# The experts' down products with the weights stationary and the output transposed and turned back

## Chip, cores and metric

The kernel runs on one core of one Trainium2 chip. The metric is device time in microseconds (us) of one execution; a kernel's time is the median of its runs. TensorE is called PE, VectorE DVE, ScalarE ACT, GpSimd POOL and SyncE SP.

## The reference, cut to what matters

The whole network is a graph convolution, a mixture of experts, an attention over edges and a second small mixture, on 10,000 tokens of 512 numbers. The change touches the first mixture only. There each of 32 experts takes the 312 tokens (k) that rank highest for it, and four experts share one up matrix:

```python
k = min(int(bs * C_CAP) // E, bs)                      # 10000 // 32 = 312
G_ek, idx_ek = jax.lax.top_k(Sm.T, k)
tokens = xf[idx_ek]
up = jnp.einsum('gjkh,ghf->gjkf', tok_g, W_up) + b_up[:, None, None, :]
act = jax.nn.silu(up).reshape(E, k, D_FF)              # D_FF = 1365
Eout = jnp.einsum('ekf,efh->ekh', act, W_down) + b_down[:, None, :]
weighted = G_ek[..., None] * Eout
y = jnp.zeros((bs, H), dtype=x.dtype).at[idx_ek.reshape(-1)].add(weighted.reshape(-1, H))
```

## The kernel before

`experts` works through the experts one after another. The 312 tokens of an expert are held as three parts (Q = 3) of 104 (S), the 512 features as four chunks (C = 4) of 128, and the 1365 hidden features as eleven tiles (M = 11), ten of 128 and one of 85. Every product is made of three matmuls, since each operand is split into a high and a low part.

The engines run their own loops and meet by semaphores. `tiles` gives each engine a list of stages with a lag; eight experts at the start and some at the end are written out, and twenty in the middle run in a hardware loop of four experts to a pass, five passes.

For an expert e the work on each engine is:

- PE: `up(e)`: for each hidden tile m, 12 matmuls with `up_hi` or `up_lo` stationary and 312 tokens moving, into one of U = 3 buffers of `psU`. Then `down(e)`: for each m, 9 matmuls with 104 tokens of `hid_hi` or `hid_lo` stationary and 512 features of `dn_hi` or `dn_lo` moving, into `psO`, which holds the three parts. Down is cut into B = 4 batches of hidden tiles (3, 3, 3, 2); behind each of the first three comes one `turn` of the next expert, which transposes 104 gathered tokens into `psT`, a tile of two buffers.
- ACT: `raise_parts(e+1)` makes `x_hi` and `dn_hi` for the next expert during `down(e)`; the `dn_hi` of a batch waits for this expert's down products of that batch, the last one for the end of down. Then `activate(e+1)`: two SiLU activations per hidden tile, one to `hid_hi`, one to `hid`.
- DVE: `lower_parts(e+1)` makes `x_lo` and `dn_lo` behind ACT; then `locate(e+2)`, eight small instructions in a chain that find the token numbers of a later expert; then `weigh(e)`, which reads `psO`, adds the bias `bdn` (the expert's row copied to all partitions) and multiplies by the gate; then `split(e+1)`, eleven subtractions that make `hid_lo`.
- POOL issues the gathers of tokens and the scatter of `y`; SP issues the loads of weights, and of `bdn`, one per expert.

The order on DVE is set by the list of stages alone, `[(0, stage), (2, prepare), (2, lower_parts), (1, locate), (3, weigh), (2, split)]`, and is strict. ACT waits before tile m for `hid_low` of tile m - 4, as `hid` has four buffers. PE waits before up tile m for the activations of tile m - U.

Of the kernel before, what the change touches and what calls it, by code (L numbers as in the profile page):

```python
# [10 lines left out]
ALU = mybir.AluOpType  # L11
# [1171 lines left out]
def experts(nc, g, K, tile_of, rest, row, W_up, b_up, W_down, b_down):  # L1183
# [14 lines left out]
    width = [min(P, F - m * P) for m in range(M)]  # L1198
    U = 3
    L = 2 * Q + 2  # L1200
# [8 lines left out]
    with Phase(nc, "experts") as ph:  # L1209
# [8 lines left out]
        bup = ph.sb("bup", [P, X // GR, M])  # L1218
        bdn = ph.sb("bdn", [P, 2, D])
        y = ph.sb("y", [P, 2, Q, D])  # L1220
# [12 lines left out]
        psU = ph.ps("psU", [P, U, 512])  # L1233
        psO = ph.ps("psO", [P, Q, 512])
        gm, gx, scattered = ph.sems("gm", 2), ph.sems("gx", 2), ph.sems("scattered", 2)
        up_loaded, dn_loaded, bias_loaded, biases = ph.sems("up_loaded", C), ph.sems("dn_loaded", 2), \
            ph.sems("bias_loaded", 2), ph.sem("biases")
        staged, located, turned, x_high, x_low, up_high, up_low, dn_high, dn_low, upped, activated = (
# [5 lines left out]
        @block.sync  # L1244
        def _(sp):
            for m in range(M):
                sp.dma_start(bup[0:width[m], :, m:m + 1],
                             b_up[:, m * P:m * P + width[m]].rearrange("g (p o) -> p g o", o=1),
                             allow_slow_non_contiguous=True).then_inc(biases, 16)
            up_rows = W_up.rearrange("g h f -> (g h) f")  # L1250
            down_rows = W_down.rearrange("e f h -> (e f) h")

            def load(e, j):
                if j == 0:
                    for c in range(C):
                        if not isinstance(e, int) or e >= GR:
                            sp.wait_ge(up_low, (e - GR) * (C // GR) + c + 1)
                            sp.sem_inc(waited, 1)
                        sp.dma_start(up_raw[:, c, :], up_rows[bass.ds(e * (D // GR) + c * P, P), :])\
                            .then_inc(up_loaded[c], 16)  # L1260
                for k in range(B):
                    if not isinstance(e, int) or e * B + k >= 2:
                        sp.wait_ge(dn_low, e * B + k - 1)
                        sp.sem_inc(waited, 1)
                    whole = [m for m in batch[k] if m < FULL]
                    sp.dma_start(dn_raw[:, k % 2, 0:len(whole), :],
                                 down_rows[bass.ds(e * F + whole[0] * P, len(whole) * P), :]
                                 .rearrange("(m p) h -> p m h", p=P)).then_inc(dn_loaded[k % 2], 16)
                    if batch[k][-1] == M - 1:
                        sp.dma_start(dn_raw[0:width[-1], k % 2, len(whole), :],  # L1270
                                     down_rows[bass.ds(e * F + FULL * P, F - FULL * P), :]).then_inc(dn_loaded[k % 2], 16)
                at_least(sp, out_step, e, 2, 2 * Q)
                sp.sem_inc(waited, 1)
                sp.dma_start(bdn[:, j % 2, :], b_down[bass.ds(e, 1), :].rearrange("o h -> (o h)").partition_broadcast(P))\
                    .then_inc(bias_loaded[j % 2], 16)
            tiles(sp, X, [(0, load)], R)

        @block.gpsimd
        def _(pool):
# [20 lines left out]
            def scatter(e, j):  # L1300


                at_least(pool, out_step, e, 0, 2 * Q)
                pair_landed(pool, scattered, e, j, Q, 1)
# [9 lines left out]
        def _(pe):  # L1314
            def turn(e, j, q):

                if q == 0:
                    pair_landed(pe, gx, e, j, Q)
                if not isinstance(e, int) or e * Q + q >= 2:
                    pe.wait_ge(x_low, e * Q + q - 1)  # L1320
                for c in range(C):
                    mm = pe.transpose(psT[:, (j * Q + q) % 2, c * S:(c + 1) * S],
                                      xg[0:S, j % 2, q, c * P:(c + 1) * P], g.ident[0:S, 0:S])
                mm.then_inc(turned, 1)

            def up(e, j):
# [4 lines left out]
                for m in range(M):  # L1331
# [3 lines left out]
                    for c in range(C):  # L1335
                        pe.matmul(acc, up_hi[:, c, cols], x_hi[:, c, :], start=(c == 0), stop=False)  # L1336
                        pe.matmul(acc, up_hi[:, c, cols], x_lo[:, c, :], start=False, stop=False)  # L1337
                        mm = pe.matmul(acc, up_lo[:, c, cols], x_hi[:, c, :], start=False, stop=(c == C - 1))  # L1338
                    mm.then_inc(upped, 1)

            def down(e, j):
                at_least(pe, out_step, e, 1, 2 * Q)
                for k in range(B):
                    pe.wait_ge(dn_low, e * B + k + 1)
                    for m in batch[k]:
                        pe.wait_ge(hid_low, e * M + m + 1)
                        w = width[m]
                        for q in range(Q):
                            s = slice(q * S, (q + 1) * S)
                            pe.matmul(psO[0:S, q, :], hid_hi[0:w, m, s], dn_hi[0:w, m, :], start=(m == 0), stop=False)  # L1350
                            pe.matmul(psO[0:S, q, :], hid_hi[0:w, m, s], dn_lo[0:w, m, :], start=False, stop=False)  # L1351
                            mm = pe.matmul(psO[0:S, q, :], hid_lo[0:w, m, s], dn_hi[0:w, m, :],  # L1352
                                           start=False, stop=(m == M - 1))
                        mm.then_inc(downed, 1)
                    if k < Q and not (isinstance(e, int) and e == X - 1):
                        turn(e + 1, (j + 1) % R, k)
            for q in range(Q):
                turn(0, 0, q)
            tiles(pe, X, [(1, up), (1, down)], R)

        @block.scalar
        def _(act):
# [10 lines left out]
            def raise_parts(e, j):  # L1373


                for k in range(B):
# [5 lines left out]
                    if not isinstance(e, int) or e >= 1:  # L1382
                        act.wait_ge(downed, (e - 1) * M + batch[k][-1] + 1)
                    act.copy(dn_hi[:, batch[k][0]:batch[k][-1] + 1, :], dn_raw[:, k % 2, 0:len(batch[k]), :])\  # L1384
                        .then_inc(dn_high, 1)

            def activate(e, j):

                for m in range(M):
# [4 lines left out]
                    if not isinstance(e, int) or e >= 1:  # L1394
# [4 lines left out]
                                   bias=bup[0:width[m], bass.ds(e // GR, 1), m]).then_inc(activated, 1)  # L1399
            tiles(act, X, [(0, prepare), (0, raise_parts), (0, activate)], R)  # L1400

        @block.vector
        def _(v):
            chain = Chain(v, located, L)
            outs = Chain(v, out_step, 2 * Q)

# [12 lines left out]
            def locate(e, j):  # L1419
                chain.at(e)  # L1420
                pair_landed(v, gm, e, j, Q)
                pair_landed(v, scattered, e, j, Q, 4)
                at_least(v, out_step, e, R, 2 * Q)
                for q in range(Q):
# [8 lines left out]
                chain.end()  # L1433

            def weigh(e, j):
                k = j % 2
                outs.at(e)
                pair_landed(v, bias_loaded, e, j, 1)
                pair_landed(v, scattered, e, j, Q, 2)
                at_least(v, downed, e, 0, M)  # L1440
                for q in range(Q):
                    outs(v.tensor_tensor(y[0:S, k, q, :], psO[0:S, q, :], bdn[0:S, k, :], ALU.add))
                    outs(v.tensor_scalar(y[0:S, k, q, :], y[0:S, k, q, :], gate[0:S, j, q:q + 1], None, ALU.mult))  # L1443
                outs.end()
# [14 lines left out]
            def split(e, j):  # L1459

                for m in range(M):
# [754 lines left out]
```

## Time and profile before

| | us |
|---|---|
| median of 3 runs | 4214.27 (4212.77 to 4214.78) |
| the profiled execution | 4210.74 |
| its span, first to last instruction | 4209.0 |
| PE busy | 3413.8 (81%) |
| DVE busy | 2659.6 (63%) |
| POOL busy | 1414.7 (34%) |
| ACT busy | 1239.1 (29%) |
| mean granted clock of PE | 0.89 |

The profile's page gives busy times by engine, the span in 40 slices of equal length, and groups of instructions by line. The trace behind it gives the start and duration of each instruction, what ended the idle time ahead of it, and sums over any stretch. A granted clock of 1.00 is PE's upper level, 2.4 GHz, and 0.50 its lower, 1.2 GHz; a value between is a mean over a stretch that has both. Durations of matmuls are modelled and overlap; the distance of their starts tells what one costs in a stream. `experts` is the stretch from about 1690 to 3110 us.

### The profile page before, as it was taken

Reading aid. Unit: us, or ns where it says so; the run is one execution under the profiler, and the core shown is the slowest. Engines: PE = TensorE matmul, PEld = TensorE weight load, DVE = VectorE, ACT = ScalarE, POOL = GpSimd, SP = SyncE. Lnnn points to the kernel's source line nnn. Section 1 sums busy time; section 2 is a strip of 40 time slices with the busy share of each in tenths; the row PEclk is TensorE's granted clock in tenths of the full one; section 3 lists DMA queues with packets and bytes.
Section 4 is the critical chain, followed back from the end, with each engine's and each line's share of the span. In section 5 each row is a group of like instructions: output and inputs, shape, how many; then the busy total and the mean of one; then the engine's idle time right before and its main releaser. Section 6 shows DMA issues by size and latency. Waiting matters only on the chain. (4 is left out here: it accounts for less than half of the span.)

```text
span 4209.0 us, 60863 instructions
## 1 busy us (share of the span) xinstructions
PE 3413.8 (81%) x16811; PEld 2667.0 (63%) x16812; DVE 2659.6 (63%) x6025; ACT 1239.1 (29%) x2287; POOL 1414.7 (34%) x1753
## 2 busy tenths in 40 slices
PE   4876377888877410899999999999949996688999
PEld 3610255666677410788888888888838884575766
DVE  7765797894367677454544545445428887776776
ACT  0122144452211100443443434344311111113443
POOL 0176387783255201132222222223113330006552
PEclk9999699999955555899999999999979998798999
DMA  1043222333399401454544534445322210126664
GB/s 51 0 126 80 63 93 83 110 97 120 118 310 310 150 0 36 131 143 102 144 124 113 134 102 137 128 107 142 95 71 60 58 55 17 74 94 147 160 156 107
DMA packets 254792, 457.41 MB, mean 109 GB/s; under 512 B 66065, under 2 KB 71482, under 8 KB 254064
## 3 DMA queue, kind: packets, MB, share of 16 engines
q1 hardware_dynamic: 180899, 288.95, 20.9%
q0 software_dynamic: 62368, 145.38, 15.8%
q10 hardware_dynamic: 11318, 20.54, 1.3%
q8 instruction: 104, 1.70, 0.2%
q14 instruction: 103, 0.84, 0.1%
HBM read 327.73 MB, written 126.85 MB: 108 GB/s over the span
## 5 line engine op out<-in xcount | busy, mean ns | idle before, releaser
L1336 PE MATMUL experts_psU<-experts_x_hi,experts_up_hi 128*128 128x312 f32 (+1 forms) x1408 | 436.8, 310 | 15.4 <-issue 11.8
L1337 PE MATMUL experts_psU<-experts_x_lo,experts_up_hi 128*128 128x312 f32 (+1 forms) x1408 | 436.6, 310 | 0.0
L1338 PE MATMUL experts_psU<-experts_x_hi,experts_up_lo 128*128 128x312 f32 (+1 forms) x1408 | 435.9, 310 | 0.0
L1350 PE MATMUL experts_psO<-experts_dn_hi,experts_hid_hi 128*104 128x512 f32 (+1 forms) x1056 | 421.5, 399 | 0.0
L1351 PE MATMUL experts_psO<-experts_dn_lo,experts_hid_hi 128*104 128x512 f32 (+1 forms) x1056 | 415.4, 393 | 0.0
L1352 PE MATMUL experts_psO<-experts_dn_hi,experts_hid_lo 128*104 128x512 f32 (+1 forms) x1056 | 415.4, 393 | 0.0
L1296 POOL DMA_INDIRECT experts_xg<-xn,experts_token_i x96 | 100.6, 1048 | 768.6 <-DVE experts_token_i L1432 749.1
L1464 DVE TENSOR_TENSOR experts_hid_lo<-experts_hid,experts_hid_hi 128x312 fp32r<-128x312 f32 (+1 forms) x352 | 161.6, 482 | 231.5 <-ACT experts_hid L1398 228.2
L1456 DVE TENSOR_TENSOR experts_dn_lo<-experts_dn_raw,experts_dn_hi 128x1536 fp32r<-128x1536 f32 (+1 forms) x128 | 207.9, 1624 | 122.5 <-ACT experts_dn_hi L1384 122.5
L1336 PEld LDWEIGHTS experts_psU<-experts_x_hi,experts_up_hi 128*128 128x128 f32 (+1 forms) x1408 | 265.4, 188 | 19.3 <-issue 17.3
L1396 ACT ACTIVATE experts_hid_hi<-experts_psU,experts_bup 128x312 fp32r<-128x312 f32 (+1 forms) x352 | 183.7, 522 | 296.7 <-PE experts_psU L1338 260.3
L1451 DVE TENSOR_TENSOR experts_x_lo<-experts_psT,experts_x_hi 128x416 fp32r<-128x416 f32 x96 | 56.7, 591 | 335.9 <-ACT experts_x_hi L1379 335.9
L1337 PEld LDWEIGHTS experts_psU<-experts_x_lo,experts_up_hi 128*128 128x128 f32 (+1 forms) x1408 | 265.3, 188 | 1.1
L1338 PEld LDWEIGHTS experts_psU<-experts_x_hi,experts_up_lo 128*128 128x128 f32 (+1 forms) x1408 | 265.2, 188 | 0.0
L1352 PEld LDWEIGHTS experts_psO<-experts_dn_hi,experts_hid_lo 128*104 128x104 f32 (+1 forms) x1056 | 177.0, 168 | 67.3
L1351 PEld LDWEIGHTS experts_psO<-experts_dn_lo,experts_hid_hi 128*104 128x104 f32 (+1 forms) x1056 | 177.7, 168 | 59.2
L1350 PEld LDWEIGHTS experts_psO<-experts_dn_hi,experts_hid_hi 128*104 128x104 f32 (+1 forms) x1056 | 177.4, 168 | 59.6
L718 PE MATMUL gcn_psZ<-gcn_wa_hi,gcn_agg_hi 128*128 128x512 f32 x480 | 201.1, 419 | 14.6 <-DVE gcn_agg_lo L821 14.5
L821 DVE TENSOR_TENSOR gcn_agg_lo<-gcn_agg,gcn_agg_hi 128x512 fp32r<-128x512 f32 x120 | 206.7, 1722 | 8.4 <-DVE gcn_mv L135 3.8
L1384 ACT CAST experts_dn_hi<-experts_dn_raw 128x1536 fp32r<-128x1536 f32 (+1 forms) x128 | 175.9, 1374 | 78.2 <-PE experts_psO L1352 72.5
L815 DVE SCALAR_TENSOR_TENSOR gcn_agg<-gnn_link,gcn_agg,gcn_psA 128x128 f32<-128x128 f32 (+1 forms) x468 | 130.5, 338 | 104.6 <-PE gcn_psA L706 104.4
L1307 POOL DMA_INDIRECT x<-experts_y,experts_token_i x96 | 161.5, 1683 | 97.6 <-DVE experts_y L1443 67.9
(391 smaller groups left out, 8506.9 us busy)
## 6 DMA issues: line engine op xcount, KB each, us to landing
experts_dn_raw<-in_L_ffn_W_down SPq DMA_DIRECT2D x96, 768.0 KB, 4.6
experts_up_raw<-in_L_ffn_W_up SPq DMA_DIRECT2D x32, 682.5 KB, 10.0
conv<-gcn_diff SPq DMA_DIRECT2D x80, 256.0 KB, 2.0
stats_xt<-in_x SPq DMA_DIRECT2D x78, 256.0 KB, 2.7
route_xt<-in_x SPq DMA_DIRECT2D x78, 256.0 KB, 4.8
x<-route_xt SPq DMA_DIRECT2D x78, 256.0 KB, 4.3
xn<-route_xn ACTq DMA_DIRECT2D x78, 256.0 KB, 4.8
two_xt<-x SPq DMA_DIRECT2D x78, 256.0 KB, 2.8
```

The source lines that it names most:

```text
L718: pe.matmul(psZ[:, j % 2, :], agg_hi[:, j, h, :], wa_hi[:, h, :], start=(h == 0), stop=False)
L821: v.tensor_tensor(agg_lo[:, j, :, :], agg[:, j, :, :], agg_hi[:, j, :, :], ALU.subtract).then_inc(low, 1)
L1336: pe.matmul(acc, up_hi[:, c, cols], x_hi[:, c, :], start=(c == 0), stop=False)
L1337: pe.matmul(acc, up_hi[:, c, cols], x_lo[:, c, :], start=False, stop=False)
L1338: mm = pe.matmul(acc, up_lo[:, c, cols], x_hi[:, c, :], start=False, stop=(c == C - 1))
L1350: pe.matmul(psO[0:S, q, :], hid_hi[0:w, m, s], dn_hi[0:w, m, :], start=(m == 0), stop=False)
L1351: pe.matmul(psO[0:S, q, :], hid_hi[0:w, m, s], dn_lo[0:w, m, :], start=False, stop=False)
L1352: mm = pe.matmul(psO[0:S, q, :], hid_lo[0:w, m, s], dn_hi[0:w, m, :], start=False, stop=(m == M - 1))
L1384: act.copy(dn_hi[:, batch[k][0]:batch[k][-1] + 1, :], dn_raw[:, k % 2, 0:len(batch[k]), :])\
L1396: act.activation(hid_hi[0:width[m], m, :], psU[0:width[m], m % U, 0:K], ACT.Silu, bias=bup[0:width[m], bass.ds(e // GR, 1), m])
L1456: v.tensor_tensor(dn_lo[:, ms, :], dn_raw[:, k % 2, 0:len(batch[k]), :], dn_hi[:, ms, :], ALU.subtract).then_inc(dn_low, 1)
L1464: v.tensor_tensor(hid_lo[0:w, m, :], hid[0:w, n, :], hid_hi[0:w, m, :], ALU.subtract)\
```

## The change

The down products are turned round. The stationary operand is now 128 features of `dn_hi` or `dn_lo`, the moving one the 312 tokens of `hid_hi` or `hid_lo`; the output is transposed, 128 features by 312 tokens for each of four chunks, in `psY`, which takes four banks where `psO` took three. For this U falls from 3 to 2.

A new stage, `lift`, copies the transposed output to `yT` and adds the bias of each feature, two chunks on ACT and two on DVE. The biases of all experts are loaded once and transposed on PE ahead of the loop. `turn_back` transposes `yT` to tokens by features again, with 12 PE transposes into `psT`, and stands in `up` of the next expert after its second tile. `psT` has two buffers and there are three parts, so part 2 waits until DVE has weighed part 0. `weigh` is now one multiplication per part, out of `psT`.

```diff
-    U = 3
+    U = 2
+    HALF = C // 2
...
-        psO = ph.ps("psO", [P, Q, 512])
+        psY = ph.ps("psY", [P, C, 512])
...
+            sp.dma_start(bdn[:, :], b_down).then_inc(down_bias, 16)
...
-                at_least(sp, out_step, e, 2, 2 * Q)
-                sp.sem_inc(waited, 1)
-                sp.dma_start(bdn[:, j % 2, :], b_down[bass.ds(e, 1), :].rearrange("o h -> (o h)").partition_broadcast(P))\
-                    .then_inc(bias_loaded[j % 2], 16)
...
@@ tensor: turn, up, down @@
+                at_least(pe, out_step, e, 2, Q)
...
+                    if m == 1 and (not isinstance(e, int) or e >= 1):
+                        turn_back(e - 1)
+
+            def turn_back(e):
+
+                pe.wait_ge(lifted_act, (e + 1) * HALF)
+                pe.wait_ge(lifted_dve, (e + 1) * (C - HALF))
+                for q in range(Q):
+                    if q >= 2:
+                        pe.wait_ge(out_step, e * Q + q - 1)
+                    for c in range(C):
+                        mm = pe.transpose(psT[0:S, q % 2, c * P:(c + 1) * P], yT[:, c, q * S:(q + 1) * S], g.ident[:, :])
+                    mm.then_inc(out_turned, 1)
...
-                        for q in range(Q):
-                            s = slice(q * S, (q + 1) * S)
-                            pe.matmul(psO[0:S, q, :], hid_hi[0:w, m, s], dn_hi[0:w, m, :], start=(m == 0), stop=False)
-                            pe.matmul(psO[0:S, q, :], hid_hi[0:w, m, s], dn_lo[0:w, m, :], start=False, stop=False)
-                            mm = pe.matmul(psO[0:S, q, :], hid_lo[0:w, m, s], dn_hi[0:w, m, :],
-                                           start=False, stop=(m == M - 1))
+                        for c in range(C):
+                            acc, cols = psY[:, c, 0:K], slice(c * P, (c + 1) * P)
+                            pe.matmul(acc, dn_hi[0:w, m, cols], hid_hi[0:w, m, :], start=(m == 0), stop=False)
+                            pe.matmul(acc, dn_hi[0:w, m, cols], hid_lo[0:w, m, :], start=False, stop=False)
+                            mm = pe.matmul(acc, dn_lo[0:w, m, cols], hid_hi[0:w, m, :], start=False, stop=(m == M - 1))
...
+            pe.wait_ge(down_bias, 16)
+            for c in range(C):
+                mm = pe.transpose(psY[:, 0, c * X:(c + 1) * X], bdn[:, c * P:(c + 1) * P], g.ident[0:X, 0:X])
+            mm.then_inc(bias_turned, 1)
...
@@ scalar @@
+            def lift(e, j):
+
+                at_least(act, downed, e, 0, M)
+                at_least(act, out_turned, e, 1, Q)
...
+                for c in range(HALF):
+                    act.activation(yT[:, c, :], psY[:, c, 0:K], ACT.Identity, bias=bdnT[:, c, bass.ds(e, 1)])\
+                        .then_inc(lifted_act, 1)
...
-            tiles(act, X, [(0, prepare), (0, raise_parts), (0, activate)], R)
+            tiles(act, X, [(0, prepare), (0, raise_parts), (1, lift), (0, activate)], R)
...
@@ vector @@
+            def lift(e, j):
+
+                at_least(v, downed, e, 0, M)
+                at_least(v, out_turned, e, 1, Q)
+                for c in range(HALF, C):
+                    v.tensor_scalar(yT[:, c, :], psY[:, c, 0:K], bdnT[:, c, bass.ds(e, 1)], None, ALU.add)\
+                        .then_inc(lifted_dve, 1)
...
-                    outs(v.tensor_tensor(y[0:S, k, q, :], psO[0:S, q, :], bdn[0:S, k, :], ALU.add))
-                    outs(v.tensor_scalar(y[0:S, k, q, :], y[0:S, k, q, :], gate[0:S, j, q:q + 1], None, ALU.mult))
+                    v.wait_ge(out_turned, e * Q + q + 1)
+                    v.sem_inc(waited, 1)
+                    outs.go(v.tensor_scalar(y[0:S, k, q, :], psT[0:S, q % 2, :], gate[0:S, j, q:q + 1], None, ALU.mult))
...
-            tiles(v, X, [(0, stage), (2, prepare), (2, lower_parts), (1, locate), (3, weigh), (2, split)], R)
+            tiles(v, X, [(0, stage), (2, prepare), (2, lower_parts), (3, lift), (1, locate), (3, weigh), (2, split)], R)
```

On DVE, between the end of an expert's down products and the next expert's `split`, this stands before (L1456 is `lower_parts`, L1425 to L1432 `locate`, L1442 and L1443 `weigh`):

```order
L1456 TENSOR_TENSOR experts_dn_lo<-experts_dn_raw,experts_dn_hi 128x1024
L1425 TENSOR_SCALAR experts_junk,experts_place<-experts_mk,ffn_rest 104x128
...
L1430 SCALAR_TENSOR_TENSOR experts_token<-ffn_tile_of,experts_place 104x3
L1432 CAST experts_token_i<-experts_token 104x3
L1442 TENSOR_TENSOR experts_y<-experts_psO,experts_bdn 104x512
L1443 TENSOR_SCALAR experts_y<-experts_y,experts_gate 104x512
```

And this after (L1471 is `lift`, L1456 to L1463 `locate`, L1481 `weigh`, L1502 `split`):

```order
L1494 TENSOR_TENSOR experts_dn_lo<-experts_dn_raw,experts_dn_hi 128x1024
L1471 TENSOR_SCALAR experts_yT<-experts_psY,experts_bdnT 128x312 x2
L1456 TENSOR_SCALAR experts_junk,experts_place<-experts_mk,ffn_rest 104x128
L1458 SCALAR_TENSOR_TENSOR experts_junk,experts_gate<-all_count,experts_place,experts_mk 104x128
...
L1461 SCALAR_TENSOR_TENSOR experts_token<-ffn_tile_of,experts_place 104x3
L1463 CAST experts_token_i<-experts_token 104x3
L1481 TENSOR_SCALAR experts_y<-experts_psT,experts_gate 104x512 x3
L1502 TENSOR_TENSOR experts_hid_lo<-experts_hid,experts_hid_hi 128x312 x10
```

The lift stands ahead of `locate`, the weighing still behind it.

On PE, inside the up products of an expert, the second tile is followed by the third before:

```order
L1336 MATMUL experts_psU<-experts_x_hi,experts_up_hi 128x312
L1337 MATMUL experts_psU<-experts_x_lo,experts_up_hi 128x312
L1338 MATMUL experts_psU<-experts_x_hi,experts_up_lo 128x312
L1336 MATMUL experts_psU<-experts_x_hi,experts_up_hi 128x312
L1337 MATMUL experts_psU<-experts_x_lo,experts_up_hi 128x312
```

And after, the twelve transposes of the previous expert's output lie between the two tiles (L1353 is `turn_back`):

```order
L1338 MATMUL experts_psU<-experts_x_hi,experts_up_hi 128x312
L1339 MATMUL experts_psU<-experts_x_lo,experts_up_hi 128x312
L1340 MATMUL experts_psU<-experts_x_hi,experts_up_lo 128x312
L1353 MATMUL experts_psT<-all_ident,experts_yT 104x128 x12
L1338 MATMUL experts_psU<-experts_x_hi,experts_up_hi 128x312
L1339 MATMUL experts_psU<-experts_x_lo,experts_up_hi 128x312
```

The wait for the weighing of part 0 is within the twelve, after the eighth.

## Rows read from the trace of the kernel before

**Rows 1.** The page: PE's busy time, and its slices with the granted clock.

```profile
PE 3413.8 (81%) x16811; PEld 2667.0 (63%) x16812; DVE 2659.6 (63%) x6025; ACT 1239.1 (29%) x2287; POOL 1414.7 (34%) x1753
...
PE   4876377888877410899999999999949996688999
...
PEclk9999699999955555899999999999979998798999
```

**Rows 2.** Window: stretch and length, busy per engine (PE to POOL), PEclk, DMA.

```profile
1690.00:3110.00 1420.00, 1388.63 (x7773) 1182.50 (x7771) 660.03 (x1261) 578.83 (x959) 352.86 (x276) 0.98 0.44 119
```

**Rows 3.** Timeline of PE: start, duration, engine, line, names, idle before it.

```profile
2305.11 0.52 PE L1322 MATMUL experts_psT<-all_ident,experts_xg 104*128 104x104 f32 x4
2305.41 0.46 PE L1350 MATMUL experts_psO<-experts_dn_hi,experts_hid_hi 128*104 128x512 f32 x1
...
2309.65 0.31 PE L1336 MATMUL experts_psU<-experts_x_hi,experts_up_hi 128*128 128x312 f32 x1
...
2328.62 0.39 PE L1350 MATMUL experts_psO<-experts_dn_hi,experts_hid_hi 128*104 128x512 f32 x1
...
2355.58 0.62 PE L1336 MATMUL experts_psU<-experts_x_hi,experts_up_hi 128*128 128x312 f32 x1 [2.80 <-issue]
...
2377.24 0.39 PE L1350 MATMUL experts_psO<-experts_dn_hi,experts_hid_hi 128*104 128x512 f32 x1
...
2401.23 0.31 PE L1336 MATMUL experts_psU<-experts_x_hi,experts_up_hi 128*128 128x312 f32 x1
```

**Rows 4.** Timeline of PE in a later stage with 128-column transposes.

```profile
3244.01 1.03 PE L1546 MATMUL score_psT<-all_ident,score_xn 128*128 128x128 f32 x8
3244.80 0.48 PE L1558 MATMUL score_psP<-score_w_hi,score_x_hi 128*128 128x512 f32 x1
```

**Rows 5.** Timeline of ACT after the down products that end at 2309.65.

```profile
2309.90 1.05 ACT L1384 CAST experts_dn_hi<-experts_dn_raw 128x1024 fp32r<-128x1024 f32 x1 [2.35 <-PE experts_psO L1352]
2311.85 0.52 ACT L1396 ACTIVATE experts_hid_hi<-experts_psU,experts_bup 128x312 fp32r<-128x312 f32 x1 [0.90 <-PE experts_psU L1338]
2312.27 0.52 ACT L1398 ACTIVATE experts_hid<-experts_psU,experts_bup 128x312 f32<-128x312 f32 x1
```

**Rows 6.** Timeline of DVE in the same stretch.

```profile
2310.98 1.23 DVE L1456 TENSOR_TENSOR experts_dn_lo<-experts_dn_raw,experts_dn_hi 128x1024 fp32r<-128x1024 f32 x1 [1.64 <-ACT experts_dn_hi L1384]
2312.13 0.34 DVE L1425 TENSOR_SCALAR_CACHE_REDUCE experts_junk<-experts_mk,ffn_rest 104x128 f32<-104x128 f32 x1
...
2315.48 0.69 DVE L1442 TENSOR_TENSOR experts_y<-experts_psO,experts_bdn 104x512 f32<-104x512 f32 x1 [0.28 <-DVE experts_token_i L1432]
...
2319.33 2.11 DVE L1464 TENSOR_TENSOR experts_hid_lo<-experts_hid,experts_hid_hi 128x312 fp32r<-128x312 f32 x5
```

**Rows 7.** Groups of DVE that read PSUM: busy us, mean ns, idle before.

```profile
L337 DVE TENSOR_TENSOR index_prod<-index_psL,index_is_lo 128x256 f32<-128x256 f32 x40 | 16.6, 415 | 0.0
L785 DVE COPY gcn_v<-gcn_psV 1x512 f32<-1x512 f32 x3 | 2.0, 679 | 3.1 <-PE gcn_psV L696 3.1
```

**Rows 8.** Windows: the four loop heads, two stalls elsewhere, one stretch with short waits.

```profile
2174.00:2186.00 12.00, 8.96 (x47) 8.07 (x46) 9.33 (x24) 2.91 (x5) 2.94 (x3) 0.86 0.99 373
2351.00:2363.00 12.00, 9.20 (x41) 8.43 (x40) 8.94 (x23) 2.83 (x5) 3.21 (x3) 0.72 0.98 375
2529.00:2541.00 12.00, 8.83 (x41) 8.19 (x40) 8.63 (x24) 2.91 (x5) 3.45 (x4) 0.72 1.01 384
2706.00:2718.00 12.00, 9.23 (x42) 8.40 (x41) 9.16 (x23) 2.73 (x5) 3.04 (x3) 0.72 0.99 376
752.00:764.00 12.00, 8.76 (x44) 6.50 (x43) 8.93 (x26) 4.46 (x11) 4.70 (x7) 1.00 0.42 111
967.00:979.00 12.00, 8.74 (x37) 6.57 (x37) 8.44 (x26) 3.74 (x9) 5.77 (x9) 0.86 0.37 111
545.00:697.00 152.00, 117.06 (x567) 87.75 (x567) 142.80 (x266) 66.91 (x134) 129.67 (x135) 1.00 0.29 93
```

**Rows 9.** The page's group of PE's weight loads for the up products.

```profile
L1336 PEld LDWEIGHTS experts_psU<-experts_x_hi,experts_up_hi 128*128 128x128 f32 (+1 forms) x1408 | 265.4, 188 | 19.3 <-issue 17.3
```

More of the change, by code:

```diff
@@ L1218, in experts @@
         bup = ph.sb("bup", [P, X // GR, M])
-        bdn = ph.sb("bdn", [P, 2, D])
+        bdn = ph.sb("bdn", [X, D])
+        bdnT = ph.sb("bdnT", [P, C, X])
+        yT = ph.sb("yT", [P, C, K])
         y = ph.sb("y", [P, 2, Q, D])
@@ L1233, in experts @@
         psU = ph.ps("psU", [P, U, 512])
-        psO = ph.ps("psO", [P, Q, 512])
+        psY = ph.ps("psY", [P, C, 512])
         gm, gx, scattered = ph.sems("gm", 2), ph.sems("gx", 2), ph.sems("scattered", 2)
-        up_loaded, dn_loaded, bias_loaded, biases = ph.sems("up_loaded", C), ph.sems("dn_loaded", 2), \
-            ph.sems("bias_loaded", 2), ph.sem("biases")
+        up_loaded, dn_loaded, biases = ph.sems("up_loaded", C), ph.sems("dn_loaded", 2), ph.sem("biases")
+        down_bias, bias_turned, bias_ready, lifted_act, lifted_dve, out_turned = (
+            ph.sem(n) for n in ("down_bias", "bias_turned", "bias_ready", "lifted_act", "lifted_dve", "out_turned"))
         staged, located, turned, x_high, x_low, up_high, up_low, dn_high, dn_low, upped, activated = (
@@ L1300, in scatter @@
             def scatter(e, j):
-                at_least(pool, out_step, e, 0, 2 * Q)
+                at_least(pool, out_step, e, 0, Q)
                 pair_landed(pool, scattered, e, j, Q, 1)
@@ L1339, in up @@
                     mm.then_inc(upped, 1)
+                    if m == 1 and (not isinstance(e, int) or e >= 1):
[9 more added lines that the diff above has]
+                    mm.then_inc(out_turned, 1)
             def down(e, j):
-                at_least(pe, out_step, e, 1, 2 * Q)
+                at_least(pe, lifted_act, e, 1, HALF)
+                at_least(pe, lifted_dve, e, 1, C - HALF)
                 for k in range(B):
@@ L1356, in down @@
                         turn(e + 1, (j + 1) % R, k)
+            pe.wait_ge(down_bias, 16)
+            for c in range(C):
+                mm = pe.transpose(psY[:, 0, c * X:(c + 1) * X], bdn[:, c * P:(c + 1) * P], g.ident[0:X, 0:X])
+            mm.then_inc(bias_turned, 1)
             for q in range(Q):
                 turn(0, 0, q)
+            pe.wait_ge(bias_ready, 1)
             tiles(pe, X, [(1, up), (1, down)], R)
+            turn_back(X - 1)
         @block.scalar
@@ L1385, in raise_parts @@
                         .then_inc(dn_high, 1)
+            def lift(e, j):
+                at_least(act, downed, e, 0, M)
+                at_least(act, out_turned, e, 1, Q)
+                if isinstance(e, int) and e == 0:
+                    act.wait_ge(bias_ready, 1)
+                for c in range(HALF):
+                    act.activation(yT[:, c, :], psY[:, c, 0:K], ACT.Identity, bias=bdnT[:, c, bass.ds(e, 1)])\
+                        .then_inc(lifted_act, 1)
             def activate(e, j):
@@ L1404, in _ @@
             chain = Chain(v, located, L)
-            outs = Chain(v, out_step, 2 * Q)
+            outs = Chain(v, out_step, Q)
             def stage(e, j):
@@ L1422, in locate @@
                 pair_landed(v, scattered, e, j, Q, 4)
-                at_least(v, out_step, e, R, 2 * Q)
+                at_least(v, out_step, e, R, Q)
                 for q in range(Q):
@@ L1465, in split @@
                         .then_inc(hid_low, 1)
-            tiles(v, X, [(0, stage), (2, prepare), (2, lower_parts), (1, locate), (3, weigh), (2, split)], R)
+            v.wait_ge(bias_turned, 1)
+            v.tensor_copy(bdnT[:, :, :].rearrange("p c e -> p (c e)"), psY[:, 0, 0:C * X]).then_inc(bias_ready, 1)
+            v.wait_ge(bias_ready, 1)
+            tiles(v, X, [(0, stage), (2, prepare), (2, lower_parts), (3, lift), (1, locate), (3, weigh), (2, split)], R)
 def attention_scores(nc, g, H, Wqkv, bqkv, score, value):
```

2 lines of the change are left out of this document (removed).

## Prediction

> **What bounds the kernel now.** I read the page's busy shares and its forty slices first [rows 1]: TensorE (PE) is busy 81% of the span, and in slices 18 to 29 it stands at 9 throughout, at a clock digit of 9. That is `experts`, and the window over it says the same: from 1690 to 3110 us PE is busy 1388.6 of 1420 us at a mean granted clock of 0.98, while DVE has 660 and ACT 579 [rows 2]. So about a third of the time hangs on one engine, and each microsecond put on or taken from PE's stream there counts in full. DVE, ACT and the transfers only matter where PE waits for them.
>
> Next I read PE's timeline for the rhythm [rows 3]. The column to watch is the start of each row, since the durations are modelled and overlap. The up products of one expert start at 2309.65 and its down products at 2328.62: 132 matmuls in 18.97 us, 0.1437 us each for 312 columns. A down phase lasts from 2377.24 to 2401.23, 23.99 us, for 99 matmuls of 512 columns and three token turns of four transposes. The turns take about 1.1 us, since one from 2305.11 to 2305.41 costs 0.30 us and makes its follower late; that leaves 22.9 us, 0.231 each. One expert is 42.96 us, and the time is 32 of them.
>
> **Down products turned round.** Per expert 11 x 4 x 3 = 132 matmuls of 312 columns replace 99 of 512. Their form (128 rows, 128 stationary columns, 312 moving) is just that of the up products, so I take the up pitch: 132 x 0.1437 = 18.97 us against 22.9. Gain 3.9 us, 32 times: **-125 us**. The bounds are narrow, 3.7 to 4.1, because the form is in the trace 4224 times. The Trainium skill ("TensorE: Matmul & The Clock Gate", Back-to-back issue gap) says that in a real stream the spacing is set by load and matmul together, about 81 ns for 128 columns and 131 for 512. Drawn in a straight line to 312 that is an estimate of 105 ns, and the turned form would be 132 x 0.105 = 13.9 us against 99 x 0.131 = 13.0, so 0.9 us dearer per expert rather than 3.9 cheaper. The trace does not agree: its 512 columns start every 231 ns, and its 312 every 144.
>
> **Turning back.** Each expert but the last gets 12 transposes with 128 moving columns, after the second up tile of the next. Eight such transposes in another stage go from 3244.01 to 3244.80, 0.099 us each, and the matmul behind them is 0.08 late [rows 4]: 12 x 0.099 + 0.08 = 1.3 us. 31 times, all on PE's path: **+40 us**. (The nearest cheaper row, the 104-column turn, would give 0.9 us; +28.)
>
> **The wait within it.** The transposes write `psT`, which has two buffers, and there are three parts (q = 0, 1, 2). So before part 2 PE waits for DVE to have weighed part 0, and the rest of the up products are queued behind that wait. When DVE gets there follows from the DVE and ACT rows of one expert [rows 5, 6]; t = 0 is the first up matmul, 2309.65.
> - ACT: `dn_hi` of the last batch runs from 0.25 to 1.30 as now. Two lifts follow at the activations' pitch of 0.42 (2311.85, 2312.27): done at 2.3. The first activation then starts near 2.3 instead of 2.20.
> - DVE: `dn_lo` of the last batch starts at 1.33, and the next instruction at 2.48. The two lifts read 312 columns of PSUM; 256 take 415 ns and 512 take 679 [rows 7], so 0.47, at the pitch of 0.41 that five 312-column subtractions show (2.11 us for five [rows 6]). They end at 3.3 to 3.4.
> - PE has done two tiles at 24 x 0.1437 = 3.45. The first wait of the turn-back costs nothing. Parts 0 and 1 are out at 3.85 and 4.25.
> - DVE has `locate` between the lift and the weighing, as the order shows. Before, from its first instruction to the first weighing are 3.35 us (2312.13 to 2315.48), a chain in which each waits for the one before. So the weighing starts at 3.3 + 3.35 = 6.65 and part 0 is done 0.68 later (a 512-column read of PSUM), at 7.33.
> - PE starts part 2 at 7.4 and the third tile at 7.9, where it was 3.45. Of these 4.45 us 1.3 are the transposes, and **3.15 us are idle**.
>
> For this to vanish, DVE would have to be 3.1 us earlier. Bounds: 2.6, if the PSUM reads cost what SBUF ones do and `locate` has no start-up; 3.7, if each hand-over takes 0.1 to 0.2 more. Four experts escape it: at the loop's heads PE stands still anyway for 2.8 us before up (2355.58, "issue" [rows 3]) while DVE goes on, and then runs slowly. 27 x 3.15 = **+85 us**.
>
> **The clock behind the wait.** Windows of 12 us around the four loop heads [rows 8] have PE busy for 8.96, 9.20, 8.83 and 9.23 us, so stalls of 2.8 to 3.2 us, and the clock in them is 0.86, 0.72, 0.72 and 0.72. The lower level is half, 1.2 instead of 2.4 GHz; so PE had it for 3.4 us once and 6.7 us three times. What this costs stands in rows 3: the up products from 2355.58 to 2377.24 take 21.66 us, 2.7 more than 18.97. In the case with 3.4 us of low clock the loss is 3.4 x (1 - 0.1437/0.26) = 1.5, with 312/1.2 = 260 ns as the slow pitch. Mean of the four: 2.4 us. Elsewhere in the trace one stall of 3.24 us kept the clock (the window at 752, clock 1.00) and one of 3.26 did not (at 967, 0.86), so five of six fell. Between 545 and 697 us PE waits often but, busy 117 of 152 us, never long, and the clock is 1.00. I take 2.2 us per stall, between 5/6 x 2.4 and 2.4; it can be 0 to 2.7. 27 times: **+59 us**.
>
> **The rest.** `psU` goes from three buffers to two. A tile takes PE 1.72 us; ACT starts 0.48 after its end (2311.85 against 2309.65 + 1.72) and needs 0.94, done at 1.42, so 0.3 is left and I put it at nothing; if that cover is gone, see below. The bias transfers leave SP's queue, where nobody waited for them. Weighing falls from six DVE instructions of 3.85 us (2315.48 to 2319.33) to three of 2; nobody on PE waited for their end, and it frees DVE only behind the stall. Down gets 3.9 us shorter; PE did not wait at its end for the next expert's tokens (no idle stands at 2401.23 [rows 3]), and the last batch, in which their chain ends, only shrinks from 18 x 0.231 = 4.2 to 24 x 0.1437 = 3.4 us. The bias setup ahead and the last turn-back behind: +1, at most +3.
>
> Sum: -125 + 40 + 85 + 59 + 1 = **+60 us**. The profiled execution (span 4209.0, time 4210.7) would be 4271; the median of the runs lies 3.5 above it, so **4274 us**.
>
> **Rivals.**
> - The wait comes as reckoned but the clock stays up: +1, so 4215. The stall at 752 speaks for it, the four in this very stream against it.
> - Two buffers of `psU` are too few, because the load of the next tile's weights wants its release earlier than the matmul: 0.1 us for each of nine tiles x 32 = 29 more, 4303. It decides if a hand-over takes over 0.3 us.
> - The other side, faster: DVE reaches the weighing well before PE needs it, so the stall is under 1.5 us and, like the waits between 545 and 697, costs no clock. At 1.5 us: -125 + 40 + 40 + 1 = -44, 4170; with none 4130. It would need `locate` or its waits to be half as long as its rows; the order gives no way.
> - The weight loads set the pitch of the down products: a load of 128 columns takes 188 ns [rows 9], 132 x 0.188 = 24.8 us, 5.8 more per expert, 4460. The up products, which load as much and start every 144 ns, speak against it.
>
> **How the numbers follow.** Forecast 0.72; clock stays 0.08; too few buffers 0.10; short stall 0.08; loads and anything else 0.02. Predicted is the first, 4274. Its own spread: clock loss from 5/6 x 1.5 to 2.7 per stall is -25 to +14 us, stall length from 2.6 to 3.7 is -15 to +15. The range of 4225 to 4320 holds these together, the too few buffers, and half-way to a clock that often stays. About 0.2%, 8 us, is what a measurement here can tell from no change. Faster by more: the short stall and a little of the clock case, 0.10; within: 0.06; slower: 0.84.
>
> **What would show it.** In the profile after: down phases of 20.1 us; a gap on PE of about 3.1 us in 27 up phases, before part 2 of the turn-back, released by DVE's weighing; half clock after most of them; an expert of about 45.7 us instead of 43.0; no gap at the loop heads beyond the one of now. I am wrong if DVE weighs before `locate` is through, if the gap is there but the clock digit of the stage stays at 9 with no window of an expert under 1.00, or if gaps stand before each up tile.

## The result, and the profile after

The changed kernel takes 4259.8 us (median of 3 runs, 4257.3 to 4263.7) where the kernel before takes 4214.3. The ratio is 1.0117, 95% interval 1.0103 to 1.0132, so it is slower by 1.2%. Forecast were 4274 us and a range of 4225 to 4320. The profiled execution has a span of 4255.6 us against 4209.0.

The window over the stage answers to [rows 2]. The columns are the stretch, its length, the busy time of PE, PE's weight loads, DVE, ACT and POOL, then PEclk, DMA share and GB/s. The further lines are up phases of single experts: one of the usual kind, one of the three that kept the clock, one with the long loss, and that of the last expert.

```profile
1690.00:3155.00 1465.00, 1352.64 (x9216) 1336.19 (x9216) 646.41 (x1228) 603.99 (x1022) 359.05 (x276) 0.96 0.41 109
1744.20:1768.80 24.60, 22.18 (x146) 21.73 (x145) 11.71 (x31) 11.09 (x23) 9.37 (x6) 0.93 0.50 117
1922.60:1945.70 23.10, 20.68 (x146) 20.23 (x146) 11.69 (x31) 11.09 (x23) 9.31 (x6) 1.00 0.54 125
2144.20:2170.40 26.20, 23.37 (x147) 22.91 (x146) 11.73 (x31) 11.20 (x23) 8.00 (x6) 0.87 0.45 110
...
3103.60:3124.80 21.20, 20.69 (x146) 20.24 (x146) 9.32 (x17) 11.09 (x23) 4.81 (x3) 1.00 0.24 31
```

PE has 36 us less work in the stage (1352.6 against 1388.6) and 112 us of idle time against 31. An up phase took 18.97 us before; now it takes 23.1 with the clock up, 24.6 usually and 26.2 at worst, while the last expert's takes 21.2. The gain is in the down phases: 20.1 us each where it was 24.0. This is PE's timeline of one expert, for [rows 3]; read the start times, and the idle time in brackets.

```profile
2308.63 0.31 PE L1366 MATMUL experts_psY<-experts_hid_hi,experts_dn_hi 128*128 128x312 f32 x1
...
2328.73 0.31 PE L1338 MATMUL experts_psU<-experts_x_hi,experts_up_hi 128*128 128x312 f32 x1
...
2332.34 1.05 PE L1353 MATMUL experts_psT<-all_ident,experts_yT 128*104 128x128 f32 x8
2336.23 0.65 PE L1353 MATMUL experts_psT<-all_ident,experts_yT 128*104 128x128 f32 x4 [2.83 <-DVE experts_y L1481]
...
2352.25 0.31 PE L1366 MATMUL experts_psY<-experts_hid_hi,experts_dn_hi 128*128 128x312 f32 x1
```

The down phase lasts from 2308.63 to 2328.73, 20.10 us where it was 23.99. Then PE does two up tiles, eight transposes, and stands still for 2.83 us until DVE has weighed part 0. DVE's timeline of the same stretch answers to [rows 6].

```profile
2330.07 1.23 DVE L1494 TENSOR_TENSOR experts_dn_lo<-experts_dn_raw,experts_dn_hi 128x1024 fp32r<-128x1024 f32 x1 [0.93 <-ACT experts_dn_hi L1405]
2331.21 0.99 DVE L1471 TENSOR_SCALAR experts_yT<-experts_psY,experts_bdnT 128x312 f32<-128x312 f32 x2
2332.11 0.34 DVE L1456 TENSOR_SCALAR_CACHE_REDUCE experts_junk<-experts_mk,ffn_rest 104x128 f32<-104x128 f32 x1
...
2335.00 0.17 DVE L1463 CAST experts_token_i<-experts_token 104x3 int32<-104x3 f32 x1
...
2335.42 1.41 DVE L1481 TENSOR_SCALAR experts_y<-experts_psT,experts_gate 104x512 f32<-104x512 f32 x2 [0.25 <-DVE experts_token_i L1463]
2337.03 0.75 DVE L1481 TENSOR_SCALAR experts_y<-experts_psT,experts_gate 104x512 f32<-104x512 f32 x1 [0.19 <-PE experts_psT L1353]
```

The lift ends at 2332.2, PE's part 0 is in `psT` by about 2332.9 (an estimate, four transposes from 2332.34), but the chain of `locate` holds DVE from 2332.11, and the weighing starts at 2335.42. Over the stage the group of the transposes shows what that adds up to.

```profile
L1353 PE MATMUL experts_psT<-all_ident,experts_yT 128*104 128x128 f32 x384 | 62.7, 306 | 74.1 <-DVE experts_y L1481 72.9 <-DVE experts_yT L1471 1.2
```

72.9 us of idle time wait for the weighing, and only 1.2 for the lift. At the loop heads, for [rows 8], the windows of 12 us (three of the four heads) and PE's rows at the first are:

```profile
2370.00:2382.00 12.00, 7.12 (x39) 6.76 (x38) 6.48 (x19) 3.77 (x6) 1.94 (x2) 0.86 1.00 371
2554.00:2566.00 12.00, 7.21 (x40) 6.85 (x39) 6.59 (x19) 3.88 (x6) 1.83 (x2) 0.86 1.01 370
2738.00:2750.00 12.00, 7.49 (x41) 7.13 (x40) 6.85 (x19) 4.15 (x6) 1.56 (x2) 0.86 0.98 364
```

```profile
2194.83 0.41 PE L1338 MATMUL experts_psU<-experts_x_hi,experts_up_hi 128*128 128x312 f32 x1 [4.19 <-issue]
2200.48 0.31 PE L1340 MATMUL experts_psU<-experts_x_hi,experts_up_lo 128*128 128x312 f32 x1 [0.99 <-issue]
...
2202.73 0.65 PE L1353 MATMUL experts_psT<-all_ident,experts_yT 128*104 128x128 f32 x4 [0.64 <-DVE experts_y L1481]
```

PE idles 4.2 us there instead of 2.8 to 3.2, and again for 1 us inside the second tile. The wait for the weighing is 0.64.

From the phase starts in the two traces the difference of the stage, 45 us of the 46.6 by which the span grew, adds up as follows.

| | us |
|---|---|
| 32 down phases, 20.10 against 23.99 | -124.5 |
| 26 ordinary up phases, mean 24.79 against 18.97 | +151 |
| four experts at loop heads: 48.1 against 48.4 us for down and the next up, so 0.35 less, with the 3.9 of down counted above | +14 |
| first up (+1.9), last up (+2.2), last turn-back (+0.6) | +5 |

Within the 151 us: the three up phases that kept the clock take 23.35 us on average, 19 with low clock for 3.4 us take 24.73, and four with 6.8 us take 26.14. The clock thus costs 26 x 1.44 = 37 us; the rest, 4.37 us each, is transposes and wait. Which phases lose the clock changes from one execution to the next.

### The profile page after: what moved, and what is told of

Read it like the earlier page. It is cut to its first block and busy times, and to the rows that moved or that the text cites. A ratio compares the mean times of both kernels' runs of the same rounds, so it can differ in the third digit from the quotient of the medians.

```text
span 4255.6 us, 63757 instructions
## 1 busy us (share of the span) xinstructions
PE 3378.8 (79%) x18256; PEld 2821.4 (66%) x18256; DVE 2648.2 (62%) x5994; ACT 1264.3 (30%) x2351; POOL 1422.8 (33%) x1753
## 5 line engine op out<-in xcount | busy, mean ns | idle before, releaser
L1338 PE MATMUL experts_psU<-experts_x_hi,experts_up_hi 128*128 128x312 f32 (+1 forms) x1408 | 453.9, 322 | 24.1 <-issue 16.1
L1366 PE MATMUL experts_psY<-experts_hid_hi,experts_dn_hi 128*128 128x312 f32 (+1 forms) x1408 | 439.1, 312 | 0.0
L1367 PE MATMUL experts_psY<-experts_hid_lo,experts_dn_hi 128*128 128x312 f32 (+1 forms) x1408 | 431.3, 306 | 0.0
L1368 PE MATMUL experts_psY<-experts_hid_hi,experts_dn_lo 128*128 128x312 f32 (+1 forms) x1408 | 429.8, 305 | 0.0
L1502 DVE TENSOR_TENSOR experts_hid_lo<-experts_hid,experts_hid_hi 128x312 fp32r<-128x312 f32 (+1 forms) x352 | 167.2, 483 | 381.2 <-ACT experts_hid L1429 381.2
L1338 PEld LDWEIGHTS experts_psU<-experts_x_hi,experts_up_hi 128*128 128x128 f32 (+1 forms) x1408 | 277.9, 197 | 29.9 <-issue 26.6
L1367 PEld LDWEIGHTS experts_psY<-experts_hid_lo,experts_dn_hi 128*128 128x128 f32 (+1 forms) x1408 | 265.5, 189 | 0.0
L1368 PEld LDWEIGHTS experts_psY<-experts_hid_hi,experts_dn_lo 128*128 128x128 f32 (+1 forms) x1408 | 265.4, 188 | 0.0
L1366 PEld LDWEIGHTS experts_psY<-experts_hid_hi,experts_dn_hi 128*128 128x128 f32 (+1 forms) x1408 | 264.9, 188 | 0.0
L1287 POOL DMA_INDIRECT experts_mk<-marks,experts_row_i x96 | 108.8, 1133 | 363.5 <-DVE experts_row_i L1440 283.9
L1599 PE MATMUL score_psP<-score_w_hi,score_x_hi 128*128 128x512 f32 x480 | 194.2, 405 | 0.0
```

The costliest lines, as they stand in the source:

```text
L1366: pe.matmul(acc, dn_hi[0:w, m, cols], hid_hi[0:w, m, :], start=(m == 0), stop=False)
L1367: pe.matmul(acc, dn_hi[0:w, m, cols], hid_lo[0:w, m, :], start=False, stop=False)
L1368: mm = pe.matmul(acc, dn_lo[0:w, m, cols], hid_hi[0:w, m, :], start=False, stop=(m == M - 1))
L1502: v.tensor_tensor(hid_lo[0:w, m, :], hid[0:w, n, :], hid_hi[0:w, m, :], ALU.subtract)\
L1599: pe.matmul(acc, hi, w_hi[:, n, c, :], start=(c == 0), stop=False)
```

## Experiments

The ratios are to the kernel before, run on the same chip in the same comparison.

**The changed kernel again.** 

> The changed kernel itself, for the comparison on the same chip: 1.012 times the kernel before, so that the part 2 version stands at 0.97 of it.

 Measured: 1.0120 (1.0103 to 1.0137), 4259.0 us against 4208.5. In this trace five of the 26 ordinary up phases kept the clock and three had 6.8 us of half clock; the mean is 24.64 us, 1.32 above those that kept it, so the clock costs 34 us in this execution. At the loop heads PE idles 3.7 to 4.3 us, and the second gap (0.7 us) stands at two of the four.

**1. The weighing ahead of `locate`.** All that changes is DVE's list.

```diff
-            tiles(v, X, [(0, stage), (2, prepare), (2, lower_parts), (3, lift), (1, locate), (3, weigh), (2, split)], R)
+            tiles(v, X, [(0, stage), (2, prepare), (2, lower_parts), (3, lift), (3, weigh), (1, locate), (2, split)], R)
```

> DVE's list with weigh ahead of locate, all else as in the changed kernel. Theory (the wait of part 2 is locate's 3.3 us on DVE, and the clock falls because of its length): the wait shrinks from 2.4 to 2.8 us to the 0.5 us that the last expert shows, where no locate stands there; the up phase falls from 24.4 to 26.2 us to about 21.2, PEclk stays at 1.00, and the time is about 4260 - 27 x (2.2 + 1.3) = 4165 us, under the kernel before (4214). Rival (the third part in two buffers costs that much by itself, through lift, hand-overs and the weighing): the wait stays near 2.5 us and the time within 10 us of 4260.

Measured: 4160.8 us, ratio 0.9892 (0.9876 to 0.9909), 2.25% or 95 us under the changed kernel (by the ratios, as for all distances below that name the changed kernel). PE's row of the wait, the window of that up phase, and DVE's weighing:

```profile
1786.27 0.65 PE L1353 MATMUL experts_psT<-all_ident,experts_yT 128*104 128x128 f32 x4 [0.53 <-DVE experts_y L1481]
```

```profile
1781.10:1802.30 21.20, 20.67 (x146) 20.22 (x146) 11.59 (x31) 11.09 (x23) 8.12 (x6) 1.00 0.53 128
```

```profile
1785.46 1.41 DVE L1481 TENSOR_SCALAR experts_y<-experts_psT,experts_gate 104x512 f32<-104x512 f32 x2 [0.93 <-PE experts_psT L1353]
```

DVE now waits for PE and not the reverse. PE idles 0.53 us, the up phase is 21.2 us, and the clock is 1.00. The cause of the wait is thereby shown: it is `locate`, and not the two buffers alone. The same stood in the changed kernel's own last expert, which has no `locate` ahead of its weighing.

**2. Part 2 turned back after the fourth tile.** `locate` stays where it is.

```diff
                     if m == 1 and (not isinstance(e, int) or e >= 1):
-                        turn_back(e - 1)
+                        turn_back(e - 1, (0, 1))
+                    if m == 3 and (not isinstance(e, int) or e >= 1):
+                        turn_back(e - 1, (2,))
...
-                for q in range(Q):
+                for q in parts:
```

> Parts 0 and 1 are turned back after the second up tile as now, part 2 after the fourth; DVE's order is unchanged, locate still ahead of weigh. Theory (only the place of PE's wait costs): the weighing of part 0 is done 7.4 us into up, the fourth tile ends at 7.9, so no wait is left, the clock stays, up is 18.97 + 1.4 = 20.4 us and the time 4260 - 27 x (2.6 + 1.4) = 4150 us. Rival (the wait goes elsewhere: split starts later on DVE, ACT waits for hid_low of tile 0 before tile 4, and with two psU buffers PE waits before tile 6): gaps of about 1 us before tile 6 and 4180 us.

Measured: 4139.0 us, 0.9841 (0.9825 to 0.9858), 116 us under the changed kernel. One up phase and the two groups of transposes in it:

```profile
1783.70:1804.40 20.70, 20.70 (x148) 20.49 (x147) 11.57 (x31) 11.10 (x23) 9.19 (x6) 1.00 0.59 138
```

```profile
1787.35 1.05 PE L1356 MATMUL experts_psT<-all_ident,experts_yT 128*104 128x128 f32 x8
1791.71 0.60 PE L1356 MATMUL experts_psT<-all_ident,experts_yT 128*104 128x128 f32 x4
```

PE is busy throughout, no idle stands ahead of either group, and the clock is up. The rival's gap before tile 6 did not come. The up phase of 20.5 us is 0.1 above 18.97 + 1.4; all that it has over 18.97 stands at the two groups of transposes. The turned form by itself is a gain.

**3. The wait filled with work.** Sixteen matmuls, whose result is not used, are put ahead of the wait for part 2.

```diff
                     if q >= 2:
+                        if not isinstance(e, int) or e < X - 1:
+                            pe.wait_ge(activated, (e + 1) * M + 1)
+                            for n in range(16):
+                                c = n % C
+                                pe.matmul(psU[:, 0, 0:K], up_hi[:, c, 0:P], x_hi[:, c, :], start=(n == 0), stop=(n == 15))
                         pe.wait_ge(out_step, e * Q + q - 1)
```

> The changed kernel with 16 more matmuls of 312 columns on PE ahead of the wait for part 2, into the psU buffer that the third tile starts anew; their result is not used. They take 2.3 us of a wait of 2.4 to 2.8. Theory (idle time makes the clock fall, and the fall costs 1.3 us per expert on average): the third tile starts as late as before, PEclk is 1.00 in nearly all experts, and the time is 4260 - 27 x 1.3 = 4225 us. Rival (the clock falls for another reason, or the loss is in the wait alone): 4260 us, with half clock behind the wait as before.

Measured: 4224.6 us, 1.0040 (1.0026 to 1.0055), 0.77% or 32 us under the changed kernel though PE does 496 matmuls more. Two up phases:

```profile
1786.90:1810.00 23.10, 22.99 (x162) 22.54 (x161) 11.66 (x31) 11.11 (x23) 9.30 (x6) 1.00 0.53 125
2046.80:2070.20 23.40, 22.91 (x162) 22.51 (x161) 11.66 (x31) 11.21 (x23) 8.83 (x6) 1.00 0.53 123
```

They last just as long as the changed kernel's three phases with the clock up (23.1 to 23.5), and here all ordinary ones do. So the wait's length and the clock are two separate costs. The second is 1.2 us per ordinary expert by the 32 us, and somewhat more by the traces, since the added matmuls themselves cost 1.6 us in the last expert and 0.7 us at each loop head. That the idle time is what brings the clock down is shown for this wait.

**4. The kernel before with two `psU` buffers.** `U = 3` becomes `U = 2`.

> The kernel before with U = 2 instead of 3, nothing else. Theory (two psU buffers suffice): about 2 us in the first expert, where ACT loads its table, and nothing in the others: 4216 us. Rival (each up tile waits about 0.1 us for its buffer, or ACT's wait for hid_low ahead of tile 4 reaches PE, which three buffers hid): 4214 + 32 x 0.5 to 1 = 4230 to 4246 us.

Measured: 4229.0 us, 1.0056 (1.0040 to 1.0073), 21 us above the kernel before on its median, 0.56% by the ratio. PE's row and ACT's rows at one tile:

```profile
1974.99 0.41 PE L1336 MATMUL experts_psU<-experts_x_hi,experts_up_hi 128*128 128x312 f32 x1 [0.81 <-ACT experts_hid L1398]
```

```profile
1971.30 0.51 ACT L1398 ACTIVATE experts_hid<-experts_psU,experts_bup 128x312 f32<-128x312 f32 x1
1974.01 0.52 ACT L1396 ACTIVATE experts_hid_hi<-experts_psU,experts_bup 128x312 fp32r<-128x312 f32 x1 [2.20 <-issue]
1974.43 0.51 ACT L1398 ACTIVATE experts_hid<-experts_psU,experts_bup 128x312 f32<-128x312 f32 x1
```

```profile
1973.35 2.10 DVE L1464 TENSOR_TENSOR experts_hid_lo<-experts_hid,experts_hid_hi 128x312 fp32r<-128x312 f32 x5
```

The rival was right. ACT's tile 4 (counted from 0) waits 2.2 us. The profile says only "issue"; by the kernel it waits there for DVE's first `hid_lo`, and DVE starts that at 1973.35, late behind `locate` and the weighing. With three buffers PE did not notice; with two it waits up to 0.8 us before its tile 6. In the changed kernel this is not seen, nor in experiments 1 and 2, where PE waits 0.53 us or not at all: outside the loop heads the starts of their up matmuls keep their distance everywhere but at the transposes. In experiment 2 ACT's tile 4 follows PE, not DVE:

```profile
1794.07 0.52 ACT L1430 ACTIVATE experts_hid_hi<-experts_psU,experts_bup 128x312 fp32r<-128x312 f32 x1 [1.23 <-PE experts_psU L1340]
```

The transposes put PE's later tiles back by 1.5 us, and DVE, with three weighings instead of six instructions, begins `hid_lo` 9.4 us into up (1793.12) where it was 9.7 [rows 6].

**5 to 7. The load of the up weights moved away from the loop head.** The kernel before, the changed one and that of experiment 2 all start 2.7 MB of loads at a loop head, 2 to 5 us before the down products there end. In SP's loop they go behind the second down batch's load, and start 3.5 to 5.5 us behind the head:

```diff
-                if j == 0:
-                    for c in range(C):
...
                 for k in range(B):
+                    if j == 0 and k == 2:
+                        for c in range(C):
...
```

> The changed kernel with the four loads of the next group's up weights (2.7 MB) issued by SP behind the first two down batches of that expert, not ahead of them: about 2.6 us after the loop head instead of 4 us ahead of it. In the changed kernel PE stands still for 4.0 to 4.2 us at each of the four loop heads and again for 0.8 to 1.1 us inside the second tile (both released by nothing that the profile shows), where the kernel before had 2.8 to 3.2 us and no second gap. Theory (PE's instructions are fetched by transfers that share the engines with this load): both gaps shrink, the first to 2 us or less, and the time falls by 4 x 3 to 5 us to about 4243. Rival (the jump back costs what it costs with a longer body): gaps of 4 us as before, time within 3 us of 4257.

Measured: 4243.8 us, 1.0096 (1.0079 to 1.0113) against 1.0120 of the changed kernel. The intervals overlap, so the 10 us stand on the traces: down and the next up take 44.7 us on average at the four heads, where they took 48.1. At the second head PE shows

```profile
2375.15 0.41 PE L1338 MATMUL experts_psU<-experts_x_hi,experts_up_hi 128*128 128x312 f32 x1 [1.44 <-issue]
2380.26 0.31 PE L1340 MATMUL experts_psU<-experts_x_hi,experts_up_lo 128*128 128x312 f32 x1 [1.97 <-issue]
```

The first gap fell from 4.0 to 1.4 us; the second, which the load now lies beside, grew from 0.9 to 2.0. The other heads have first gaps of 1.0 to 1.5 us, and two of them second ones of 1.1 and 2.0.

> The kernel before with the later load of the up weights alone. Fetch theory: its four gaps of 2.8 to 3.2 us at the loop heads, and the half clock behind them, shrink, 4208 - 4 x 3 = 4196 us. Rival: no change, 4208 us.

Measured: 4189.6 us, 0.9961 (0.9949 to 0.9974), 15 us under the kernel before. Windows at the first, second and third loop head:

```profile
2171.00:2183.00 12.00, 12.00 (x64) 9.57 (x63) 5.70 (x7) 4.04 (x6) 0.00 (x0) 1.00 0.32 94
2342.00:2354.00 12.00, 12.00 (x61) 9.32 (x60) 5.33 (x5) 4.15 (x4) 0.00 (x0) 1.00 0.30 96
2513.00:2530.00 17.00, 16.57 (x90) 13.35 (x89) 8.85 (x20) 6.69 (x9) 0.00 (x0) 1.00 0.46 157
```

Against [rows 8] the DMA share fell from 0.99 to 0.3, and at the first two heads PE is busy 12.00 of 12 us where it was 8.96 and 9.20; at the third and fourth 0.43 and 0.35 us of idle time are left. The clock is 1.00 at all four. So the load's nearness makes most of the gap: shown.

That what it delays is PE's own instructions is not shown by an experiment, but the traces have a trail of it. Among the DMA transfers they list some of the kind `instruction`, 16 KB each on queue 8. All 60 times that PE idles at a loop head for "issue", in the eleven traces together, it goes on 2.2 to 3.2 us after such a transfer has started. In the kernel before one starts at 2176.55, 0.5 us after PE has gone idle, and PE goes on at 2179.14; here one starts at 2177.24, 2.8 us ahead of the up products at 2180.04, and no gap is left. The second gap of the changed kernel ends in the same way (transfer at 2197.88, PE at 2200.48). The transfer takes 0.96 us with the load near and without, so it is its start that comes later. What holds the start back is not shown, and the trace does not name the engine that the instructions are for.

> Part 2 turned back after the fourth up tile, together with the later load of the up weights. If the fetch theory holds, the gain of both adds up: 4139 - 4 x 3 to 5 = 4120 to 4127 us. If it does not, 4139, or more if the weights now come too late for ACT and the next group's up products wait.

Measured: 4123.5 us, 0.9805 (0.9788 to 0.9821). This is experiment 2 with the later load, 131 us under the changed kernel and 2% under the kernel before; it and experiment 8 are the best of the study. First gaps of 1.0 to 1.5 us are left, and at two heads second ones of 2.1 and 2.5.

**8. The load earlier instead.** In experiment 2's kernel SP issues the loads between those of the second and third down batch of the expert before. SP runs ahead, so in time they fall into the up phase of the last expert ahead of the loop head (issued from 2116.2 to 2118.2, landed at 2131.2, with the head at 2154.8), some 33 us earlier than in the kernel before and not 10 as expected.

```diff
...
+                    if j == 3 and k == 2 and not (isinstance(e, int) and e == X - 1):
+                        for c in range(C):
+                            sp.wait_ge(up_low, (e + 1 - GR) * (C // GR) + c + 1)
...
```

> Part 2 turned back after the fourth up tile, and the next group's up weights loaded between the second and the third down batch of the expert before, some 10 us earlier than in the kernel before, so that they have landed ahead of the loop head. Fetch theory: the gaps at the loop heads are as short as where no load of up weights is near (0.4 us, as in the kernel before with the later load), the second gap is gone, and the time is 4 x 2 to 4 us under the 4123 us of the later load: 4107 to 4115 us. Rival (a rest of 1.0 to 1.5 us is the longer body's own): 4120 to 4125 us.

Measured: 4126.8 us, 0.9804 (0.9787 to 0.9820), equal to the later load. The rival holds: a gap of 1.0 to 1.4 us is left at each head of the longer body with no load of up weights near it, as here at the second, and a second one of 1.4 us at the fourth.

```profile
2319.70 0.41 PE L1340 MATMUL experts_psU<-experts_x_hi,experts_up_hi 128*128 128x312 f32 x1 [1.01 <-issue]
```

At these heads the instruction transfer starts 1.6 to 1.7 us before PE goes idle; in the shorter body of experiment 7 it starts 2.2 us before where a gap is left (0.4 us), and 2.8 to 3.1 us ahead of the up products where none is. What sets that start, and so why the longer body keeps this rest, stays open. At the first of these heads a gap of 1.19 us had 3.4 us of half clock behind it; at the other three none followed.

## Why the prediction was right, point by point

**Down products: -125, measured -124.5.** The pitch of the up form held: 20.10 us less 1.1 for turns is 19.0 for 132 matmuls. The straight line drawn from the Trainium skill ("TensorE: Matmul & The Clock Gate", Back-to-back issue gap), by which the turned form would have cost more, did not hold here: its estimate for 312 columns was 105 ns, and the turned products start every 144. Nor did the rival of the weight loads.

**Turning back and the wait: 4.45 us per expert, measured 4.37.** The schedule came as reckoned: the first wait costs next to nothing (1.2 us in the whole stage), the weighing starts 6.69 us after the first up matmul (2335.42 against 2328.73) where 6.65 was put, and experiment 1 shows that `locate` is what holds it. The wait misses the four loop heads nearly (0.64 us each). It misses the last expert too, which the step overlooked: there is no `locate` there, so 26 experts wait and not 27. That expert's up phase grew by 2.2 us and not 4.45, and it lost no clock. The trace shows 2.4 us (nine experts) to 2.8 us as idle, not 3.15: it counts from the modelled end of the eight transposes (2332.34 + 1.05), which lies 0.3 us behind 8 x 0.099 from their start. The sum of both terms is not touched by that.

**The clock: +59, measured +37.** The mechanism was right, and experiment 3 isolates it. The size was off: 23 of 26 waits brought half clock, as forecast, but 19 of them for 3.4 us and only four for 6.8, where the loop heads of before had three of four at 6.8 [rows 8]. A loss of 1.4 us and one of 2.8 average 1.44 over all 26; I had taken 2.2, for 27. This term alone is 22 us too high, more than the whole distance between 4274 and 4260; that the number came out nearer is luck, as the loop heads below cost 9 us more. It also explains the expert of 44.9 us where 45.7 was forecast.

**The loop heads: put at nothing more than the transposes, measured +9 beyond.** I assumed that the gap would stay at 2.8 us. It is 4.0 to 4.2 with a second of 0.8 to 1.1 and the 0.64 of the weighing, less some of the clock's loss. So "no gap at the loop heads beyond the one of now" failed. Experiments 5 to 7 show that both gaps depend on the load of the up weights beside them.

**Two buffers: put at nothing, right for this kernel, for another reason.** I counted only the hand-over from PE to ACT and back, 0.3 us of slack. I left out that ACT's tile 4 waits for DVE (the 2.2 us of experiment 4). Alone it costs 21 us. Here it is seen only in the first expert (1.9 us); in the others the transposes come in between, and experiment 2 shows no gap there even where PE does not wait for the weighing.

**The rest**, +1, was 0.6 at the end and 1.9 in the first expert. The table's sum, -124.5 + 151 + 14 + 5, is the 45 us of the stage; 1 us more of the span lies outside it.

## What to carry to other kernels

A turned product that saves columns gave its 4 us per expert in full, and the way back cost more than that, through one in-order engine: before putting a wait into the bound engine's stream, follow what stands on the other engine's list ahead of what it waits for, and move either the work or the wait. Swapping two entries of DVE's list was worth 95 us, and moving four transposes two tiles later 116; each took the kernel from 1.2% slower than before to faster. A wait on TensorE is paid again in clock, here half as much on top (1.4 us on 2.4 to 2.8), and a spare buffer that looks idle may be covering a third engine's lateness.

## What the runs showed that I had not expected

- A stall of TensorE at a loop head, which the profile ascribes to nothing, depends on large transfers near it: 2.8 to 3.2 us, with half clock behind, beside a load of 2.7 MB (DMA share 0.99), and 0 to 0.4 us when it was started some 8 us later (share 0.3 at the first two heads). That alone takes 0.4% off the kernel before. The stall ends each time 2.2 to 3.2 us after the start of a 16 KB instruction transfer.
- With the longer loop body, 1.0 to 1.5 us remain there whether the load is moved later or earlier.
- 496 unused matmuls in a wait made the kernel 32 us faster, by the clock that they kept.
